# A BitNet feed-forward on one Trainium2 core: row statistics by ScalarE passes, no clips, the row-tile loop one tile deeper

## What is computed

```python
x = x + jnp.tanh(g_ffn[3]) * _L3_ffn_ref(_layernorm(x), w1, b1, gamma, beta, w2, b2)

# B, S, D, F = (4, 512, 512, 2048)
def activation_quant(x):
    scale = 127.0 / jnp.clip(jnp.max(jnp.abs(x), axis=-1, keepdims=True), EPS, None)
    return jnp.clip(jnp.round(x * scale), -128.0, 127.0) / scale
def bitlinear(x, w, b):
    return jnp.einsum('bsd,fd->bsf', activation_quant(x), weight_quant(w)) + b
h = bitlinear(x, w1, b1)
h = jax.nn.gelu(h, approximate=False)
h = layernorm(h, gamma, beta)          # over the 2048 columns of a row
return bitlinear(h, w2, b2)
```

## Time and profile before

| | us |
|---|---|
| three runs, median (lowest, highest) | 4227.35 (4224.88, 4228.24) |
| the profiled execution, its own time | 4230.01 |
| its span in the trace | 4228.4 |
| first transpose of the stage's tiles (L1348) | starts at 3868.11 |
| last store of x issued (L546) | 4223.76 |

### The profile page before, as it was taken

The page is one execution under the profiler, slowest core; times in us unless marked ns, Lnnn a source line. Parts: engine busy times, 40 slices in busy tenths (PEclk is TensorE's granted clock), DMA queues, the critical chain, the costliest instruction groups (busy, mean ns, idle before and its releaser), DMA issues.

```text
span 4228.4 us, 41511 instructions
## 1 busy us (share of the span) xinstructions
PE 3735.9 (88%) x12786; PEld 1938.3 (46%) x12786; DVE 3070.6 (73%) x4986; ACT 1683.3 (40%) x2649; POOL 650.9 (15%) x647
## 2 busy tenths in 40 slices
PE   5989898989999988989974999899999999998656
PEld 3565655644444434434432444455454554553222
DVE  6777777768989784888898754476474673774887
ACT  5767676632322322433330011254353452551322
POOL 1333333433434110333210000000000000000000
PEclk8999999999999999999986999899999999999888
DMA  3323232424242412334422000221021120110000
GB/s 109 116 90 111 90 118 87 179 93 156 83 151 89 150 47 86 109 132 164 165 100 110 1 1 0 71 71 62 27 70 44 45 70 27 62 57 33 10 10 20
DMA packets 89971, 339.96 MB, mean 80 GB/s; under 512 B 11920, under 2 KB 20240, under 8 KB 76080
## 3 DMA queue, kind: packets, MB, share of 16 engines
q1 hardware_dynamic: 59728, 220.61, 14.6%
q0 software_dynamic: 30048, 116.94, 8.1%
HBM read 278.26 MB, written 59.24 MB: 80 GB/s over the span
## 4 chain that ended last, share of the span: by engine, by line
PE 56%; DVE 24%; issue 10%; ACT 6%; DMA 3%; DVEq 0%; POOL 0%; ACTq 0%; SPq 0%; POOLq 0%
PE ps L972 37%; PE ps L1315 5%; PE ps L1046 4%; PE ps L1305 3%; DVE room L1467 2%; PE ps L1192 2%; PE ps L1142 2%; DVE room L1471 2%; PE ps L1039 2%; DVE room L1475 1%; DMA room<-bc_scratch 1%; DVE stat L1429 1%; DVE room L1480 1%; DVE stat L1921 1%; DVE room L1926 1%
## 5 line engine op out<-in xcount | busy, mean ns | idle before, releaser
L972 PE MATMUL ps<-room 128*128 128x512 bf16 (+1 forms) x2912 | 958.5, 487 | 120.4 <-ACT room L920 45.2
L972 PE MATMUL ps<-lnT,room 128*128 128x512 f32 x2240 | 991.2, 598 | 26.3 <-DVE room L1661 11.6
L972 PEld LDWEIGHTS ps<-room 128*128 128x128 bf16 (+1 forms) x2912 | 400.2, 141 | 649.1 <-issue 325.6
L568 POOL TENSOR_TENSOR idle<-idle 128x1 f32<-128x1 f32 x288 | 459.1, 1594 | 1520.5 <-ACT room L773 572.0
L972 PEld LDWEIGHTS ps<-lnT,room 128*128 128x128 f32 x2240 | 427.1, 192 | 574.6 <-issue 533.9
L1142 PE MATMUL ps<-room 128*128 128x512 f32 x864 | 378.4, 595 | 8.5 <-DVE room L1613 8.5
L647 ACT ACTIVATE room<-room,small 128x511 f32<-128x511 f32 x256 | 163.6, 710 | 368.5 <-DVE room L1471 354.6
L972 PE MATMUL ps<-down_rows,room 128*128 128x256 f32 x1024 | 253.0, 403 | 47.0 <-ACT room L767 44.5
L1528 DVE TENSOR_TENSOR_SCAN room<-room 128x2048 f32<-128x2048 f32 x64 | 283.2, 4425 | 6.2
L1471 DVE TENSOR_TENSOR_SCAN room<-room 128x2048 f32<-128x2048 f32 x64 | 283.4, 4428 | 5.4
L1885 DVE TENSOR_REDUCE stat<-ps 128x1 f32<-128x512 f32 x256 | 177.1, 692 | 131.1 <-PE ps L972 131.1
(11 more groups left out here) (217 smaller groups left out, 4917.3 us busy)
## 6 DMA issues: line engine op xcount, KB each, us to landing
kv_stash<-room POOLq DMA_DIRECT2D x128, 256.0 KB, 2.6
room<-in_ffn SPq DMA_DIRECT2D x16, 2048.0 KB, 10.9
room<-bc_scratch POOLq DMA_DIRECT2D x128, 256.0 KB, 3.6
room<-kv_stash SPq DMA_DIRECT2D x64, 512.0 KB, 3.5
room<-stash POOLq DMA_DIRECT2D x24, 1024.0 KB, 9.1
room<-in_ffn SPq DMA_DIRECT2D x20, 1024.0 KB, 4.9
room<-in_ffn SPq DMA_DIRECT2D x12, 1536.0 KB, 8.1
room<-bc_scratch SPq DMA_DIRECT2D x64, 256.0 KB, 3.5
```

The source lines that it names most:

```text
L568: nc.gpsimd.tensor_tensor(idle[:, :], idle[:, :], idle[:, :], ALU.add).then_inc(zeros_added, 1)
L972: last = nc.tensor.matmul(out, lhsT, rhs, start=(i == 0), stop=(i == len(parts) - 1))
```

## The change

- ScalarE's GELU also sums its row (`accum_out`); a one-column pass turns the sum into minus the mean; a Square pass over the tile with that bias sums the squared deviations (its 128x2048 bf16 output `b_dev` is not read). VectorE's `normalize` takes mean and variance from there: bn_stats and bn_aggr are gone.
- Both clips are gone: since a row is scaled by 127 over its own largest magnitude, a rounded value lies within the limits. The taking off of RND for the hidden tile moves from VectorE to a second ScalarE pass (`quantize`); for x it stays on VectorE as one instruction.
- The loop is one tile deeper: TensorE does `out(u)`, `transpose_x(u+3)`, `hidden(u+3)`; ScalarE `quantize(u)`, GELU and its statistics for u+2, `take_hqT(u)`, `take_xqT(u+3)`; VectorE `bit_front` of the next batch at the beginning of step j = 2, then `final(u-2)`, `normalize(u)`.

```diff
-(b_ga0, b_ga1, b_hq, b_hqT, b_tmp) = split(arena[:, 0:H * S], F3, F3, F3 // 2, F3 // 2, D)
+(b_ga0, b_ga1, b_hq, b_hqT, b_tmp, b_dev) = split(arena[:, 0:H * S], F3, F3, F3 // 2, F3 // 2, D, F3 // 2)
-b_xq, b_xqT, b_hq, b_hqT = (v.bitcast(BF16) for v in (b_xq, b_xqT, b_hq, b_hqT))
+b_xq, b_xqT, b_hq, b_hqT, b_dev = (v.bitcast(BF16) for v in (b_xq, b_xqT, b_hq, b_hqT, b_dev))
 def psb(bank, n=1):
...
+b_mean, b_sq = sem("b_mean"), sem("b_sq")
...
         batches(act, body)
     def bitnet(stage):
-        dq1, sc2, rnd = stat[:, 116:120], stat[:, 132:134], stat[:, 134:135]
+        dq1, sc2, rnd, unrnd = stat[:, 116:120], stat[:, 132:134], stat[:, 134:135], stat[:, 135:136]
+        total, mean, squares = stat[:, 48:50], stat[:, 50:52], stat[:, 52:54]
         def take_xqT(u):
             act.wait_ge(b_xtr, u + 1)
...
             act.wait_ge(b_mm2, u)
             nc.scalar.activation(b_hqT, psb(5, 2), ACT.Copy).then_inc(b_hT_ready, 1)
-        def scale_up(u, j):
+        def gelu(u, j):
+            i = slice(j % 2, j % 2 + 1)
+            act.wait_ge(b_mm1, u + 1)
+            nc.scalar.activation(b_ga[j % 2], ps[:, 0:4, :], ACT.Gelu, scale=dq1[:, j:j + 1], accum_out=total[:, i]
+                                 ).then_inc(b_gelu, 1)
+            act.wait_ge(b_gelu, u + 1)
+            nc.scalar.activation(mean[:, i], total[:, i], ACT.Copy, scale=-1.0 / F3).then_inc(b_mean, 1)
+            act.wait_ge(b_mean, u + 1)
+            nc.scalar.activation(b_dev, b_ga[j % 2], ACT.Square, bias=mean[:, i], accum_out=squares[:, i]
+                                 ).then_inc(b_sq, 1)
+        def quantize(u, j):
             act.wait_ge(b_scale_ready, u + 1)
             nc.scalar.activation(b_ga[j % 2], b_ga[j % 2], ACT.Identity, scale=sc2[:, j % 2:j % 2 + 1], bias=rnd
                                  ).then_inc(b_round, 1)
+            act.wait_ge(b_round, u + 1)
+            act.wait_ge(b_htr, u)
+            nc.scalar.activation(b_hq, b_ga[j % 2], ACT.Identity, bias=unrnd).then_inc(b_hq_ready, 1)
         def step(batch, j, first=False, left=B * NT):
             u = batch * NT + j
-            if left > 1:
-                act.wait_ge(b_mm1, u + 2)
-                if not first:
-                    act.wait_ge(b_hq_ready, u)
-                jn = (j + 1) % NT
-                nc.scalar.activation(b_ga[jn % 2], ps[:, 0:4, :], ACT.Gelu, scale=dq1[:, jn:jn + 1]
-                                     ).then_inc(b_gelu, 1)
-            if not first:
-                take_hqT(u - 1)
-            scale_up(u, j)
+            quantize(u, j)
             if left > 2:
-                take_xqT(u + 2)
+                act.wait_ge(b_hq_ready, u + 1)
+                gelu(u + 2, (j + 2) % NT)
+            take_hqT(u)
+            if left > 3:
+                take_xqT(u + 3)
         act.wait_ge(x_done, B * stage)
         take_xqT(0)
         take_xqT(1)
-        act.wait_ge(b_mm1, 1)
-        nc.scalar.activation(b_ga[0], ps[:, 0:4, :], ACT.Gelu, scale=dq1[:, 0:1]).then_inc(b_gelu, 1)
+        gelu(0, 0)
+        take_xqT(2)
+        gelu(1, 1)
         bit_steps(act, step)
-        take_hqT(B * NT - 1)
     plan = [lambda: mamba(0), lambda: ffn(1, 0), lambda: attention1(2), lambda: ffn(3, 1),
             lambda: gate_mamba(4), lambda: ffn8(5), lambda: attention3(6), lambda: bitnet(7)]
...
         def step(batch, j, first=False, left=B * NT):
-            if not first:
-                out(u - 1)
-            if left > 2:
-                jn = (j + 2) % NT
+            out(u)
+            if left > 3:
+                jn = (j + 3) % NT
-                pe.wait_ge(b_gelu, u + 2)
-                hidden(u + 2, jn)
+                pe.wait_ge(b_gelu, u + 3)
+                hidden(u + 3, jn)
-        for u in range(2):
+        for u in range(3):
-                pe.wait_ge(b_xT_ready, 1)
+                pe.wait_ge(b_xT_ready, u)
-                pe.wait_ge(b_gelu, 1)
+                pe.wait_ge(b_gelu, u)
-        out(B * NT - 1)
...
+    v.memset(stat[:, 135:136], -RND)
...
-        link(v.tensor_scalar(b_xq, b_nx, RND - 128.0, RND, ALU.max, ALU.subtract))
-        v.tensor_scalar(b_xq, b_xq, 127.0, None, ALU.min).then_inc(b_xq_ready, 1)
-    FRONT = 3 + 11 + 2 + 2 + 1 + 3
+        v.tensor_scalar(b_xq, b_nx, RND, None, ALU.subtract).then_inc(b_xq_ready, 1)
+    FRONT = 3 + 11 + 2 + 2 + 1 + 2
     def attention3(stage):
...
     def bitnet(stage):
         def normalize(u, j):
-            ga = b_ga[j % 2]
-            st, mv, rs, tmp = stat[:, 48:72], stat[:, 72:74], stat[:, 74:75], stat[:, 76:78]
-            dve.wait_ge(b_gelu, u + 1)
-            for i in range(4):
-                ins = v.bn_stats(st[:, 6 * i:6 * i + 6], ga[:, i * 512:(i + 1) * 512])
-            link(ins)
-            v.memset(stat[:, 159:160], 0.0)
-            link(v.bn_aggr(mv, st))
-            link(v.tensor_scalar(stat[:, 75:76], mv[:, 1:2], EPS, None, ALU.add))
-            link(v.scalar_tensor_tensor(out=ga, in0=ga, scalar=mv[:, 0:1], in1=b_gamma, op0=ALU.subtract, op1=ALU.mult))
-            rsqrt(rs, stat[:, 75:76], 1, tmp)
+            ga, i = b_ga[j % 2], slice(j % 2, j % 2 + 1)
+            mean, squares = stat[:, 50:52], stat[:, 52:54]
+            rs, var, tmp = stat[:, 74:75], stat[:, 75:76], stat[:, 76:78]
+            dve.wait_ge(b_sq, u + 1)
+            link(v.tensor_scalar(var, squares[:, i], 1.0 / F3, EPS, ALU.mult, ALU.add))
+            link(v.scalar_tensor_tensor(out=ga, in0=ga, scalar=mean[:, i], in1=b_gamma, op0=ALU.add, op1=ALU.mult))
+            rsqrt(rs, var, 1, tmp)
-            row_scales(mx, sc2[:, j % 2:j % 2 + 1], dq2[:, j % 2:j % 2 + 1], bit_mean[:, 2:3]
-                       ).then_inc(b_scale_ready, 1)
-        NORMALIZE = 3 + 1 + 11 + 2 + 2
-        def clip(u, j):
-            ga = b_ga[j % 2]
-            dve.wait_ge(b_round, u + 1)
-            dve.wait_ge(b_htr, u)
-            link(v.tensor_scalar(b_hq, ga, RND - 128.0, RND, ALU.max, ALU.subtract))
-            v.tensor_scalar(b_hq, b_hq, 127.0, None, ALU.min).then_inc(b_hq_ready, 1)
+            row_scales(mx, sc2[:, i], dq2[:, i], bit_mean[:, 2:3]).then_inc(b_scale_ready, 1)
+        NORMALIZE = 2 + 11 + 2 + 2
         def final(u, j):
...
         def step(batch, j, first=False, second=False, left=B * NT):
-            if not first:
-                clip(u - 1, (j - 1) % NT)
+            if j == NT - 2 and left > NT:
+                bit_front(batch + 1)
-            if j == NT - 2 and left > NT:
-                bit_front(batch + 1)
-        n = NT * (1 + NORMALIZE + 1) + FRONT
+        n = NT * (NORMALIZE + 1) + FRONT
...
-        clip(B * NT - 1, NT - 1)
```

## The result

The changed kernel takes 4209.01 us, the median of five runs (4204.78 to 4212.98), against 4227.35 us (4224.41 to 4228.27): a ratio of 0.9958, with a 95% interval of 0.9944 to 0.9973. That is 18.3 us less, where 15.75 were forecast, and 4211.6 us was predicted. The profiled execution took 4207.69 us.

What follows compares the result with a forecast made beforehand. VectorE, with its wait for ScalarE, was the bound; the TensorE-ScalarE ring would take over. GELU(2) at 3899.9 plus 268.5 of intervals plus 44.25 ends at 4212.65, 15.75 us earlier; median 4211.6 us, range 4193 to 4231.

Steps and rivals of the forecast that it cites:

- filling the pipe: Start of the stage, before the regular intervals: GELU(1) put at 3889.95 and GELU(2) at 3899.9.
- ten plain: The ten GELU-to-GELU intervals that do not cross into the next batch, each put at 19.95 us.
- end: From the last GELU to the span's end: last statistics, product, `final`, `normalize`, `quantize` and the last tile's chain, 44.25 us.
- The ring: TensorE-ScalarE loop: `hidden`, GELU, mean, Square, copy, product, transposes; 7.09 + 6.55 + 5.15 + 1.16 = 19.95 us a tile.
- GELU to product: From GELU's start to the product's, with sum, mean, Square and copy between: 6.55 us against 3.86 before, ends 6.1 and 7.2.
- The product's clock: Cost of TensorE's longer wait: every product taken as slow, 5.15 us to the next transposes, ends 3.46 and 6.1.
- leaving `hidden` fast: TensorE's `hidden` matmuls, taken as not slowed by the longer wait: 7.09 us from `hidden` to GELU.
- The front: Across batches: GELU, VectorE's second half of the front, `final`, `normalize`, `quantize`, next GELU; 23.0 us in place of 19.95.
- No table was loaded for the Square: Rival: ScalarE switches tables for Square and back for Gelu; 4250 us, or 4231 with one load hidden; chance 0.06.
- The clock's bad case: Rival: longer waits slow both product (6.1 us) and `hidden` (another 1.4); 22.3 us a tile, 4235 us; chance 0.08.
- the full clock: Rival: TensorE's clock stays full, product in 3.46 us, 18.26 us a tile, 4195 us; chance 0.12.
- the old ring of 17.3: Rival: the Square does not delay the copy, so the TensorE-ScalarE loop stays at 17.3 us; 4185 us; chance 0.05.

Runs made afterwards that it cites:

- e10: The changed kernel with VectorE's whole front of the next batch back at its old place, behind `normalize` of tile 2: 4229.60 us.
- e1: The changed kernel with ScalarE's copy of the transposed hidden tile (`take_hqT`) moved ahead of the next GELU's mean and Square: 4179.72 us.
- e2: The changed kernel with the Square pass made twice, one behind the other: 4233.01 us.
- e3: The changed kernel with VectorE's front cut in two at its wait, the second half moved behind `normalize` of tile 2: 4208.01 us.
- e5: The changed kernel with mean and variance back on VectorE by bn_stats and bn_aggr, without GELU's sum, mean and Square passes on ScalarE: 4192.52 us.
- e9: The changed kernel with the taking off of RND for the hidden tile back on VectorE, in place of ScalarE's second quantise pass: 4218.48 us.
- e7: The kernel of e3 with 32 idle matmuls, their result unread, added in TensorE's wait before the product: 4187.37 us.
- e8: The kernel of e6 with 16 idle matmuls, their result unread, added in TensorE's wait before the product: 4157.80 us.
- e6: The kernel of e1 with the front cut in two, first half at the beginning of step j = 1, second behind `normalize` of j = 2: 4165.70 us.

## Why the prediction was right

**The sum, term by term.** From the first GELU to the end it was 21.4 (two tiles of filling the pipe) + 199.5 (ten plain) + 69.0 (three fronts) + 44.25 (end) = 334.2 us. Measured: 23.8 + 199.1 + 67.7 + 43.3 = 333.9. So the saving in the stage came out as forecast, 15.75 against 16.0 us. That it did so to 0.3 us is luck in part: the filling was 2.4 us longer, the other three terms 2.7 shorter, and in the profile of e10 the same filling took 20.6. The median fell by 18.3; the 2.3 us more are within the spread of the five runs (8.2 us), and by the moving start of the stage they can't be assigned.

**The ring.** 19.95 us predicted, 19.91 the mean. But two terms of it are off and cancel. GELU to product was put at 6.55 and is 6.2 when the missing record is counted in: 1.86 to the accumulator, 0.23 to the mean, 0.23 to the Square, 2.00 to the copy, 1.9 to the product. The accumulator's read behind the Square, put at 0.19, costs nothing: it runs under the Square's end, and the copy starts 2.00 us after the Square did. The product was too short by as much (below). The Trainium skill (ScalarE: Activation LUTs, What ACT_TABLE_LOAD costs) has about 1.99 us for an ACTIVATE of 2048 columns with a pointer bias, and 93 ns for each further pointer operand; the trace agrees, 2.002 for the Square and 2.086 for the pass with scale and bias. Where the mechanism had been only argued, e1 and e2 showed it from both sides.

**The product's clock.** I let every product be slow, 5.15 us to the next transposes. In the plain steps the rows have 6.11 for the first and 4.4 to 5.3 for the others, 5.5 in the mean with the missing 0.4 us; never 3.46, and every `hidden` from the fourth tile on at 7.05. Right in kind and 0.3 us short in size, but I had no account of what chose between them, and one premise was misread. The prediction says that only the last two tiles were slow twice. In the trace of the kernel before two of the three fronts were too: behind 14.16 and 14.77 us of waiting `hidden` took 8.44 and 8.48, and the product behind it 5.31 each time, the first of them in the row at 3957.57:

```profile
3945.30 8.44 PE L972 MATMUL ps<-room 128*128 128x512 bf16 x24 [0.78 <-ACT room L915]
```

So the ground for leaving `hidden` fast was weaker than it read, and the outcome kinder than the evidence. e3 shows that the clock is no detail: a regular ring of 20.5 us had the slowest products and swallowed 6 us of an edit that did what it should.

**The front.** 23.0 predicted, 22.57 measured, by the chain named. The wait of the product for `final` (8.03 us once, 8.07 twice) was missed; I had not followed the semaphore of PSUM bank 7. It cost nothing here, since the other chain was longer: `hidden` behind it ended at 4020.2, and the next GELU, behind ScalarE's two passes, started at 4021.45. e3 removed both at once, so what it would cost alone is open.

**The ends.** The filling took 2.4 us more than predicted. `hidden(1)`, 8.43 us before, took 10.02 after the same wait of some 4 us, and `hidden(2)` 8.31 after 3.04; in e10, with the same program so far, they took 8.45 and 6.83. The end took 1 us less: its last transposes start 28.05 us after the last GELU (27.9 predicted), and the chain from there on took 15.25 for 16.3.

**The rivals.** No table was loaded for the Square; the Trainium skill's rule that cheap functions are in every set (ScalarE: Activation LUTs, Table sets) agrees with this trace, though the page does not name Square among them. The clock's bad case, with both groups slow, came in the filling and not in the ring, and the full clock in no plain step; the old ring of 17.3 did not come either. e1 produced it on purpose, 4180 against the 4185 I had put for it.

**What the prediction did not say.** It judged the sum, not the parts. By the medians, e5 shows that one of them, as placed, took 16.5 us away, e9 that moving the second pass off VectorE gave some 9, e10 that the front's place gave some 20. They don't add up to the gain, for they interact, and they were run on other chips than the changed kernel; the kernel before stood at 4225.7 to 4227.4 us beside them.

## What to carry to other kernels

When the bound engine is relieved, look for the next ring before adding up what was saved: follow one buffer around all engines, in each engine's program order, and put every new instruction in it at its place. Passes moved to an idle engine cost nothing or all of their time by their position in its queue alone: here 29 us lay in two calls exchanged (e1), 24 of them in the ten plain steps. Where a long piece of work has a wait in the middle, put its halves where each has slack.

## What the runs showed of the hardware

- Adding matmuls that nobody reads made a kernel 20.6 us faster (e7 against e3), with the granted clock of the stretch going from 0.83 to 0.96.
- Behind the same wait of 1.95 us (e7), or of 2.93 us, the same product takes 3.63 or 5.31 us. Behind waits of 5.8 us the changed kernel's products take 5.2 to 5.6 us by their rows and e3's 5.7 to 5.8, and its plain interval is 0.6 us longer.
- The same program does not always get the same clock: behind a wait of 4.06 us `hidden(1)` took 10.02 us in the profile of the changed kernel and 8.45 in that of e10.
- An idle time of TensorE can cost more than itself, and not in proportion: `hidden`, 7.05 us otherwise, took 2.6 us more behind 6.03 us of waiting for x (e10), 2.3 more behind 2.92 (e8), 1.6 more behind 1.52 (e7), and nothing more behind 2.33 (e6).
- An accumulating ACTIVATE costs one more instruction of 0.19 us, of which 0.1 overlaps the pass: the copy starts 1.96 us after the GELU where it stood 1.86 behind it before (e1). Behind the Square it adds nothing to the 2.00 us (3961.05 to 3963.05).
